# Each search, choice and extraction of the expert choice in two units spread evenly over the steps, keys and decoding at the head of a step

## What is computed

```python
    q = (x_norm @ wq).reshape(B, T, HEADS, 2, DIM_KEY)
    sim = jnp.einsum('bthpd,hkpd->pbthk', q, keys)
    s1, i1 = jax.lax.top_k(sim[0], K)
    s2, i2 = jax.lax.top_k(sim[1], K)
    all_idx = (i1[..., :, None] * NUM_KEYS + i2[..., None, :]).reshape(B, T, HEADS, K * K)
    all_scores = (s1[..., :, None] + s2[..., None, :]).reshape(B, T, HEADS, K * K)
    final_scores, pk = jax.lax.top_k(all_scores, K)
    final_idx = jnp.take_along_axis(all_idx, pk, axis=-1)
    wd = expert_down[final_idx]
    wu = expert_up[final_idx]
    hidden = jnp.einsum('btd,bthkd->bthk', x_norm, wd)
    hidden = jax.nn.gelu(hidden, approximate=False)
    hidden = hidden * jax.nn.relu(final_scores)
    out = jnp.einsum('bthk,bthkd->btd', hidden, wu)
```

## Time and profile before

| what | value |
|---|---|
| time, median of 3 runs | 1239.93 us (1236.59 to 1240.88) |
| the profiled execution's own time | 1236.87 us |
| its span | 1235.1 us |
| PE busy | 1061.3 us (86%) |
| DVE busy | 982.2 us (80%) |
| POOL busy | 535.8 us (43%) |
| ACT busy | 392.6 us (32%) |
| chain of waits, by engine | PE 53%, DVE 26%, POOL 8%, issue 7%, DMA 3%, ACT 2%, SP 1% |

### The profile page before, as it was taken

One profiled execution on the slowest core, in us unless ns is written; L12 is line 12 of the kernel. 1 busy time (PEld: TensorE's weight loads), 2 busy tenths in 40 slices (PEclk: granted clock), 3 DMA queues, 4 the chain that ended last, 5 costly groups with the idle time before them and its releaser, 6 DMA issues.

```text
span 1235.1 us, 28831 instructions
## 1 busy us (share of the span) xinstructions
PE 1061.3 (86%) x10152; PEld 728.0 (59%) x10152; DVE 982.2 (80%) x4900; ACT 392.6 (32%) x717; POOL 535.8 (43%) x708
## 2 busy tenths in 40 slices
PE   4899987878868685148998999999999999999998
PEld 2444442323213223047777777888878888888887
DVE  4757555959999998588999999999989999964321
ACT  2256544424444361013222222222222222222211
POOL 6320410432111222226565676676766675766400
PEclk9799998888888797557999999999999999999999
DMA  5344313211321100360000000000100010000000
GB/s 167 123 140 142 114 46 121 80 54 42 92 86 41 48 11 26 108 237 2 2 29 16 16 25 16 20 27 9 40 12 25 2 34 16 25 16 24 2 18 9
DMA packets 59925, 63.76 MB, mean 52 GB/s; under 512 B 6882, under 2 KB 56164, under 8 KB 59268
## 3 DMA queue, kind: packets, MB, share of 16 engines
q1 hardware_dynamic: 59780, 61.90, 15.5%
HBM read 42.21 MB, written 19.66 MB: 50 GB/s over the span
## 4 chain that ended last, share of the span: by engine, by line
PE 53%; DVE 26%; POOL 8%; issue 7%; DMA 3%; ACT 2%; SPq 1%; POOLq 0%; DVEq 0%; ACTq 0%
PE bank L1256 50%; DVE mem L1175 4%; POOL mem L783 4%; PE bank L1259 3%; DVE mem L1111 2%; DVE mem L1212 2%; DVE mem L1058 1%; DVE mem L1057 1%; SPq L484 1%; DVE mem L1114 1%; DVE mem L1107 1%; DVE mem L1094 1%; DVE mem L1062 1%; DVE mem L1054 1%; DVE mem L979 1%
## 5 line engine op out<-in xcount | busy, mean ns | idle before, releaser
L1256 PE MATMUL bank<-mem 128*128 128x32 bf16 (+5 forms) x9672 | 1012.3, 276 | 104.2 <-DVE mem L1175 35.6
L1256 PEld LDWEIGHTS bank<-mem 128*128 128x128 bf16 (+3 forms) x9672 | 675.7, 123 | 390.0 <-issue 171.8
L783 POOL TENSOR_TENSOR mem<-mem 128x1536 bf16<-128x1536 bf16 x118 | 325.7, 2761 | 236.4 <-DVE mem L1212 202.7
L1175 DVE TENSOR_REDUCE mem<-bank 128x1 f32<-128x512 f32 x256 | 167.9, 682 | 82.1 <-PE bank L1256 81.9
L888 ACT ACTIVATE mem<-bank 128x512 f32<-128x512 f32 x256 | 148.8, 601 | 203.5 <-PE bank L1256 202.6
L924 ACT ACTIVATE bank<-bank 128x512 f32<-128x512 f32 x128 | 74.5, 582 | 332.3 <-PE bank L1256 332.3
L1212 DVE TENSOR_TENSOR mem<-mem,bank 128x2048 bf16<-128x2048 bf16 x128 | 155.4, 1214 | 0.0
L1259 PE MATMUL bank<-mem 128*128 128x128 f32 (+3 forms) x480 | 75.5, 289 | 66.2 <-POOL mem L695 25.0
L1226 DVE TENSOR_TENSOR mem<-bank,mem 128x512 f32<-128x512 f32 x128 | 87.7, 685 | 49.1 <-ACT bank L924 43.8
L1259 PEld LDWEIGHTS bank<-mem 128*128 128x128 f32 (+3 forms) x480 | 54.9, 142 | 113.5 <-issue 70.8
L932 ACT COPY mem<-bank 128x512 f32<-128x512 f32 x128 | 74.9, 585 | 113.3 <-PE bank L1256 113.3
(11 more groups left out here) (101 smaller groups left out, 678.7 us busy)
## 6 DMA issues: line engine op xcount, KB each, us to landing
mem<-parts_d SPq DMA_DIRECT2D x192, 64.0 KB, 2.3
parts_d<-mem SPq DMA_DIRECT2D x16, 384.0 KB, 2.6
mem<-in_L_ffn_expert_down SPq DMA_DIRECT2D x16, 256.0 KB, 2.8
downT_d<-mem SPq DMA_DIRECT2D x16, 256.0 KB, 3.1
mem<-downT_d SPq DMA_DIRECT2D x4, 1024.0 KB, 8.8
mem<-in_L_ffn_expert_up SPq DMA_DIRECT2D x4, 1024.0 KB, 16.0
tok_d<-mem SPq DMA_DIRECT2D x16, 160.0 KB, 1.8
mem<-tok_d SPq DMA_DIRECT2D x16, 160.0 KB, 2.5
```

Of the source, the lines that this page charges most:

```text
L783: nc.gpsimd.tensor_tensor(ow[q % 2], i0, i1, ALU.mult).then_inc(ow_rdy, 1)
L1175: nc.vector.tensor_reduce(nmx[g % 2][:, i % TB, i // TB:i // TB + 1], psum[n % 3][:, :], AX.X, ALU.max, negate=True).then_inc(s_max, 1)
L1256: return nc.tensor.matmul(o, l, r, start=first, stop=last)
```

## The change

`TASKS` has 34 entries in place of 17. A search is two: max8, index and match-replace of both sides, and the second max8 and index. A choice is two: max8 and match-replace of two heads, and the same again. An extraction is two: max8 and match-replace, and the second max8. The decoding is a task of its own. No instruction is added or taken away on any engine. `spread` lays the 34 out as before; `at_heads` then moves keys and decoding to the next step where they would share a step with a task ahead of them (unless it is the stretch's last), and what follows them goes along. In the second stage DVE does a task of that kind before the one-hots of its step. `FEW` is 10, so that the first slot holds 10 of the halves: at the steps 0, 1, 3, 4, 6, 8, 9, 11, 12 and 14, where whole searches stood at 0, 3, 6, 9 and 12. What other engines hang on a task hangs on the half that ends it (or, for `numbers`, on the half that begins choice 0).

```diff
-        TASKS = ([("search", h) for h in range(FH)] +  [("choose", s) for s in range(4)] +
-                 [("keys", 0)] + [("extract", s) for s in range(4)])
+        TASKS = ([("search", n) for n in range(2 * FH)] + [("choose", n) for n in range(8)] + [("keys", 0)] +
+                 [("extract", n) for n in range(8)] + [("decode", 0)])
+        HEAD = ("keys", "decode")
+
+        def at_heads(tasks, steps):
+
+            out = []
+            for s, t, kind, i in tasks:
+                s = max(s, out[-1][0]) if out else s
+                if kind in HEAD and out and out[-1][0] == s and s + 1 < steps:
+                    s += 1
+                out.append((s, t, kind, i))
+            return out
...
-        FEW = 5
+        FEW = 10
...
-                       "fetch": [t0 + (t + 1) for s, t, kind, i in tasks if s == x and (kind, i) == ("search", 4)],
+                       "fetch": [t0 + (t + 1) for s, t, kind, i in tasks if s == x and (kind, i) == ("search", 9)],
...
-                       "turn": [t0 + t for s, t, kind, i in tasks if s + 3 == x and (kind, i) == ("extract", 3)]}
+                       "turn": [t0 + t for s, t, kind, i in tasks if s + 3 == x and kind == "decode"]}
...
+                    rest = now["tasks"]
+                    if rest and rest[0][1] in HEAD:
+                        choose_experts(*rest[0])
+                        rest = rest[1:]
                     if on(kk, -1, 6):
                         one_hots(k, par, kk, q)
                     if on(kk1, 0, 7):
                         weigh_hidden(k1, p1, q1)
-                    for task in now["tasks"]:
+                    for task in rest:
                         choose_experts(*task)
```

More of the change, by code:

```diff
@@ L1043, in _, with search @@
             steps = Steps(dve, dve_step)
[L1045 to L1058 removed]
+            cut = []
+            def search(tile, h, second):
+                src = [sim[:, (2 * h + c) * NK:(2 * h + c + 1) * NK] for c in range(2)]
+                s, i = s16, i16.bitcast(U32)
+                if not second:
+                    if h == 0:
+                        sim_taken(dve, tile)
+                        at_least(dve, cix, tile * len(SEGS))
+                        nc.vector.tensor_copy(gate[:, 0:1], gate[:, 1:2])
+                    top = [steps.count(nc.vector.max(s[:, h, c, 0:8], src[c])) for c in range(2)]
+                    for c in range(2):
+                        steps.after(top[c])
+                        steps.count(nc.vector.max_index(i[:, h, c, 0:8], s[:, h, c, 0:8], src[c]))
+                    cut[:] = [steps.count(nc.vector.match_replace(left[c], s[:, h, c, 0:8], src[c], GONE)) for c in range(2)]
+                    return
                 top = []
@@ L1100, in make_keys, with extract @@
                 steps.count(nc.vector.tensor_tensor(ik, ik, bits(taken), ALU.bitwise_or))
-            def extract(s):
-                if s == 0:
-                    steps.all()
+            def extract(s, second):
                 both = [(k, o, h) for h in (2 * s, 2 * s + 1) for k, o in ((wkey, kA), (ikey, kB))]
-                a = [steps.count(nc.vector.max(o[:, h, 0:8], k[:, h, :])) for k, o, h in both]
-                b = []
+                if not second:
+                    if s == 0:
+                        steps.all()
+                    a = [steps.count(nc.vector.max(o[:, h, 0:8], k[:, h, :])) for k, o, h in both]
+                    cut.clear()
+                    for n, (k, o, h) in enumerate(both):
+                        steps.after(a[n])
+                        cut.append(steps.count(nc.vector.match_replace(k[:, h, :], o[:, h, 0:8], k[:, h, :], 0.0)))
+                    return
                 for n, (k, o, h) in enumerate(both):
-                    steps.after(a[n])
-                    b.append(steps.count(nc.vector.match_replace(k[:, h, :], o[:, h, 0:8], k[:, h, :], 0.0)))
-                for n, (k, o, h) in enumerate(both):
-                    steps.after(b[n])
+                    steps.after(cut[n])
                     steps.count(nc.vector.max(o[:, h, 8:16], k[:, h, :]))
```

61 lines of the change are left out of this document (26 added, 35 removed).

## The result

The changed kernel was timed three times, each time with the kernel before on the same chip:

| job | changed, median (runs) | before, median (runs) | ratio, 95% interval |
|---|---|---|---|
| first | 1256.03 us (4: 1251.72 to 1262.69) | 1240.41 us (4) | 1.0117 [1.0078, 1.0155] |
| second | 1248.99 us (12: 1241.17 to 1256.17) | 1243.89 us (35) | 1.0054 [1.0021, 1.0087] |
| third | 1249.16 us (12: 1241.43 to 1256.11) | 1242.53 us (35) | 1.0037 [1.0008, 1.0066] |

The account below looks back on a forecast made before the run. DVE was taken to bound attention and steps 16 to 47, PE the loop, a DVE-POOL-PE cycle the first slot. Terms 2.0 + 2.0 + 1.3 + 0 = +5.3 on 1239.93 gave 1245.2 us, range 1236.5 to 1250.

Parts of the forecast that it names:

- term 1: Attention stage, groups 10, 14 and 18: the wait for POOL's scale grows by 0.66 us each; +2.0, bounds 0 to 2.7.
- Term 2: First slot of the second stage: three second halves land behind the waiting one-hots, 0.66 us each; +2.0, bounds 0 to 3.3.
- Term 3: Second stage, steps 16 to 47: changed waits at gates, keys and decoding sum to +1.3 us, bounds -3 to +4.
- Term 4: Loop and last slots: PE sets the pace, so nothing is lost; 0 us, bounds 0 to +6.
- no change: Attention and first slot: the 0.66 us delays are returned, leaving +1.3 from steps 16 to 47; 1241.2 us; chance 0.27.
- Free keys: Steps 16 to 47: DVE gets the port before POOL, keys unblocked, two gates no longer wait; -6.0, 1233.9 us; chance 0.13.
- Held loop: Loop: heavy steps delay hidden weighing, PE's `output` waits 1 us in each of six tiles; 1251 us; chance 0.06.

## Why the prediction was right and wrong

- **The step that failed**: "In both the kernel goes as fast as DVE gets through its list; what counts is the sum of its work and its waits". For the attention stage that holds from the eighth reduction of a group on. The starts of the even groups are PE's, and how long they take is set by PE's clock. The prediction names such a start only as a place where 0.66 us might be returned, and puts its time at nothing, so term 1 had an upper bound of 2.7. In the three traces the stage measured +17.6, +5.2 and +15.0 to the first one-hots. In the first, the one of the job outside the range, 4.8 of them lie ahead of group 8, with no choice; 7.9 lie between the first and the eighth reduction of group 10 (30.70 us for 22.85), and 2.3, by the second trace, at the start of group 12, both at half clock. The job's other three runs have no trace. The profile before had signs of it: a clock share of 0.84 between 300 and 400.
- **Term 1, attention, +2.0**: its mechanism and its waits are shown (1.45 and 2.04). The parts in which DVE is full repeat: from the eighth reduction of group 10 to group 12, of 12 to 14 and of 14 to 15 they take 49.0, 42.2 and 21.8 us in the traces with halves, and 47.8, 41.7 and 20.5 in all eight without; from group 15 on, 105.9 or more against 105.3 or less. With 0.4 less at each undisturbed start of groups 12 and 14 (9.5 us for 9.9), that is +3.0 at the same clock. Groups 8 and 9 with the start of group 10 give back up to 0.95 in the second trace, which leaves +2.0, but they scatter by more than that. So the size is +2 to +3, under the bound of 2.7 or just over it. The three waits of 0.66 are 2.0 of it; what the rest is, if it is there, stays open.
- **Term 2, first slot, +2.0**: +1.7 in each trace, counted from the first search on (41.39 to 43.1). From one-hots to one-hots, steps 8 to 11 give +0.66, 11 to 14 +0.65, 14 to 16 +0.40: the three pairs that were forecast at 0.66 each. The pairs of steps 0 and 1, and 3 and 4, cost nothing, as forecast: steps 1 to 5 are 0.66 longer, and step 0 behind its gate is 0.66 shorter. The waits at steps 8, 11 and 14 grew by 0.37 only and not by 0.66.
- **Term 3, steps 16 to 47, +1.3**: +0.8. Gates 2.44, 1.84, 3.05 and the keys' wait of 2.2 as forecast. Heads gain, together, 1.3 us (no heads: 186.74), where the forecast's terms for them give 1.1.
- **Term 4, loop, 0**: +0.2, -1.5, -1.4. Most of this is one short fall of PE's clock in steps 80 to 87 (0.96 and 1.00 above), which the traces of before and of the first job have and the later two have not. Among all traces without it the loop takes 333.9 to 334.1 with the changed second stage and 334.3 to 334.5 with that of before. Nothing is lost there, as forecast.
- **Sum**: +5.3 forecast. Terms as measured, 2.0 to 3.0, 1.7 and 0.8, give +4.5 to +5.5; the later two jobs gave +5.1 and +6.6 between medians (ratios 1.0054 and 1.0037). That these come so near is in part luck, since their runs fall on both sides of a gap of 2.6 us and the median lies on its upper side. The range's upper end, 1250, held the upper bounds of three terms; that of the loop (+6) was left out of it, and PE's clock at the starts of the groups, 5 to 8 us in group 10 each time it comes, had no term.
- **Rivals**: no change fell (all three intervals lie above 1). Free keys fell as argued: the keys' 2.5 us came back (0.58 for 3.12), and the wait of 2.23 for POOL's numbers took them, while the gates of tiles 6 and 8 still wait. Nobody contested the port at that head. The decoding did meet a weighing, which had started 1.11 us earlier (671.21), and its first instruction ended with it, 1.73 us later. The trace agrees with the Trainium skill ("SBUF — State Buffer", Who interferes with whom) that whoever starts first blocks the other for the whole instruction. Held loop fell (4.74).

**What stays open.** Whether the halves make the half clock more frequent. Traces in which it comes, by the order of DVE ahead of the place (that of the version with halves for tiles 0 to 3 is left out, and so are those with the load held or behind small stores in group 10):

| place, and what shows it | with halves | with whole tasks |
|---|---|---|
| group 10, load in its place: 28.1 us or more to the eighth reduction, not 22.7 to 24.5 | 5 of 7 | 0 of 3 |
| group 10, early load: some 15 us at 0.50, not 3 | 2 of 3 | 0 of 2 |
| starts of groups 12 and 14: 11.2 us or more to the eighth reduction, not 9.3 to 9.9 | 7 of 22 | 12 of 16 |
| group 15, 18 to 24 us behind its first reduction: a clock of 0.50, not 0.72 to 0.75 | 5 of 11 | 0 of 8 |

The five in the last row take 108.0 us or more from the first reduction of group 15 to the first one-hots, the other six with halves 105.9 to 106.3, and those with whole tasks 105.3 or less. That stretch, before and in the second trace of the changed kernel:

```profile
431.00:437.00 6.00, 6.00 (x23) 1.86 (x26) 6.00 (x44) 1.79 (x3) 0.00 (x0) 0.72 0.01 1
```

```profile
433.00:439.00 6.00, 5.81 (x16) 1.86 (x17) 6.00 (x46) 2.36 (x4) 0.00 (x0) 0.50 0.00 1
```

So where PE's clock is low goes with the order of DVE, and in both directions: at the starts of groups 12 and 14 halves have it less often. These are few traces, and in group 10 five small stores brought it in the kernel before. The runs don't settle the sum of it either: in the two later jobs 14 of 24 runs of the changed kernel lie above 1248, and 32 of 70 of the kernel before above 1243. Nor do they tell what exactly has to coincide.

## What to carry to other kernels

Where DVE is full, moving half a task from ahead of a wait to behind it lengthens the path by just that half, and an evener spread gains nothing; a gate or a wait for POOL can be priced from the profile to a tenth of a us, the stretch that it lies in to half a us or so. But another order of work goes with other moments at which PE's clock is low, and a stretch can be 7 us longer in one run and not in the next: give such stretches a term of their own in the range, from the rows at either clock, and judge from a dozen runs in more than one job, not from four in one. When a stretch is cut for measuring, what moves over its edge has to be counted on both sides (here 0.66 us between steps 0 and 1). A DMA that a busy queue issues late (here behind thirteen loads and five stores) is worth moving ahead on its own: that gave 3 to 5 us in the kernel before.

## What the hardware showed that was not expected

- PE at 1.2 GHz for 15 us in a row while it is busy 14.28 of 15 us, and in another execution of the same kernel 2.4 GHz in the same stretch. The Trainium skill ("TensorE: Matmul & The Clock Gate", Part 1: The HAM clock gate) says that the hardware judges PE's activity in windows that run free of the kernel, so that the same kernel differs from run to run; three executions with 30.70, 22.68 and 28.14 us for one stretch agree with that; no run here shows the windows.
- Neither the length of the wait ahead of it (1.99 us with half clock, 5.91 without) nor the order of the vector engine's work (34.09 us with the old one) tells whether it comes.
- Five small stores on SP, each of 1 KB, moved the issue of the load behind them by 2.8 us (4.6 us ahead of group 10's first reduction to 1.8), and PE's wait for it from 2.29 to 7.74 us.
- A single-input decoding instruction (line 1143, 0.23 us free) took 1.73 us beside a POOL weighing under way.
